# Decoder on one core: a new order of the 16-head part's small operations, with three places behind each pair of products instead of one per slot

## What is computed

```python
def _L0_attn_ref(x, w_qkv, w_proj):
    qkv = x @ w_qkv
    ...
    q = q * cos + _rotate_half(q) * sin
    k = k * cos + _rotate_half(k) * sin
    attn = jax.nn.softmax(jnp.einsum('bhqd,bhkd->bhqk', q, k) * scale, axis=-1)
    out = jnp.einsum('bhqk,bhkd->bhqd', attn, v)
    ...
    return out @ w_proj
...
x = _layernorm(x + _L0_attn_ref(x, L0_attn_w_qkv, L0_attn_w_proj), axis=-1)
x = _layernorm(x + _L0_xattn_ref(x, ctx_1024, ctx_1024, ...), axis=-1)
```

## Time and profile before

| | |
|---|---|
| median of three runs | 2249.5 us (2247.09 to 2249.76) |
| the profiled execution | span 2234.3 us; its own device time is not listed apart from the three runs, whose median is 15.2 us over the span |
| PE busy | 2109.7 us (94%) |
| DVE, ACT, POOL busy | 1661.7, 1501.9, 1327.5 us |
| copies | 248.92 MB, mean 111 GB/s |
| chain that ended last | PE 77%, copies 5%, POOL 5%, SP's queue 4%, ACT 3%, DVE 3% |

### The profile page before, as it was taken

The page is one execution under the profiler, slowest core; times in us unless marked ns, Lnnn a source line. Parts: engine busy times, 40 slices in busy tenths (PEclk is TensorE's granted clock), DMA queues, the critical chain, the costliest instruction groups (busy, mean ns, idle before and its releaser), DMA issues.

```text
span 2234.3 us, 44819 instructions
## 1 busy us (share of the span) xinstructions
PE 2109.7 (94%) x13992; PEld 1475.9 (66%) x13992; DVE 1661.7 (74%) x3987; ACT 1501.9 (67%) x3418; POOL 1327.5 (59%) x1376
## 2 busy tenths in 40 slices
PE   3899999999999999977999999899989999998998
PEld 2544444444444444346888888788878888887887
DVE  4777888777888888747888888656388888886675
ACT  2287777777888888855777777554367777775443
POOL 0344555533334444477888877454378887875775
PEclk7699999999999999999999999999999999999999
DMA  7667677665756666434545455300055554552111
GB/s 154 109 125 147 140 146 137 144 143 124 154 136 155 159 160 137 140 101 105 131 109 115 103 115 110 93 26 6 1 138 116 111 113 107 108 114 62 58 62 43
DMA packets 201337, 248.92 MB, mean 111 GB/s; under 512 B 26584, under 2 KB 119512, under 8 KB 201112
## 3 DMA queue, kind: packets, MB, share of 16 engines
q1 hardware_dynamic: 198552, 237.68, 47.7%
q0 software_dynamic: 2560, 8.39, 1.1%
HBM read 97.47 MB, written 63.44 MB: 72 GB/s over the span
## 4 chain that ended last, share of the span: by engine, by line
PE 77%; DMA 5%; POOL 5%; SPq 4%; ACT 3%; DVE 3%; issue 2%; POOLq 0%; ACTq 0%; DVEq 0%
PE PS L485 14%; PE PS L487 12%; PE PS L486 12%; PE PS L606 9%; PE PS L590 8%; PE PS L573 5%; PE PS L699 5%; PE PS L675 5%; PE PS L684 4%; DMA KS<-hs 3%; PE PS L659 2%; SPq L1496 2%; SPq L1464 1%; ACT PT L827 1%; DMA hs<-HL 1%
## 5 line engine op out<-in xcount | busy, mean ns | idle before, releaser
L1003 DVE TENSOR_REDUCE MX<-PS 128x1 f32<-128x512 f32 x1024 | 642.5, 682 | 167.1 <-PE PS L573 156.9
L827 ACT ACTIVATE PT<-PS 128x512 f32<-128x512 f32 x1024 | 546.2, 599 | 129.5 <-PE PS L590 127.6
L573 PE MATMUL PS<-KS,QS 48*128 48x512 f32 x1024 | 357.0, 454 | 43.7 <-DMA KS<-hs 33.5
L590 PE MATMUL PS<-QS,KS 50*128 50x512 f32 x1024 | 385.5, 456 | 6.4 <-ACT PT L827 6.0
L590 PEld LDWEIGHTS PS<-QS,KS 50*128 50x128 f32 x1024 | 164.9, 187 | 270.5 <-issue 212.3
L1369 POOL TENSOR_TENSOR PB<-PB,RC 128x512 f32<-128x512 f32 (+1 forms) x256 | 250.6, 999 | 48.6 <-DVE RC L1123 48.6
L606 PE MATMUL PS<-PT,VP 128*17 128x512 f32 x2048 | 273.6, 606 | 2.9 <-ACT OT L834 2.9
L890 ACT ACTIVATE PB<-PB,NMf 128x256 f32<-128x256 f32 (+1 forms) x512 | 242.6, 478 | 8.6 <-DVE NMf L1114 8.5
L573 PEld LDWEIGHTS PS<-KS,QS 48*128 48x128 f32 x1024 | 171.5, 192 | 108.0 <-issue 59.3
L1349 POOL TENSOR_TENSOR RI<-RI,mhalf 128x8 f32<-128x8 f32 x128 | 214.1, 1672 | 10.7
L1114 DVE CUSTOM_DVE_ANT_0 PB<-PS,mk 128x256 f32<-128x256 f32 (+1 forms) x512 | 175.7, 385 | 54.4 <-PE PS L675 54.2
(11 more groups left out here) (182 smaller groups left out, 5054.4 us busy)
## 6 DMA issues: line engine op xcount, KB each, us to landing
qT<-QN SPq DMA_DIRECT2D x384, 128.0 KB, 2.4
hs<-HL SPq DMA_DIRECT2D x64, 512.0 KB, 3.8
kT<-kT SPq DMA_DIRECT2D x256, 128.0 KB, 2.5
QS<-hs SPq DMA_DIRECT2D x192, 128.0 KB, 5.9
KS<-hs SPq DMA_DIRECT2D x192, 128.0 KB, 8.0
od<-OT SPq DMA_DIRECT2D x64, 256.0 KB, 5.9
OC<-od SPq DMA_DIRECT2D x32, 256.0 KB
cst<-rs SPq DMA_DIRECT2D x32, 256.0 KB
```

The source lines that it names most:

```text
L573: pe.matmul(PS[:, bank, :], QS[rows, s, h // 2, qt * P:(qt + 1) * P], KS[rows, s, h // 2, :], start=True, stop=True).then_inc(fills("amax" ...
L590: pe.matmul(PS[:, bank, :], KS[rows, s, pair, kt * P:(kt + 1) * P], QS[rows, s, pair, :], start=True, stop=True).then_inc(fills("score", v ...
L827: act.activation(PT[:, kt % 2, 2 * i + half], PS[:, TURNS["score", vb, g, kt, half, i][0], :], ACT.Exp).then_inc(drains("score", vb, g, kt ...
L1003: dve.tensor_reduce(MX[:, vb % 2, h // 8, qt, c:c + 1], PS[:, TURNS["amax", vb, h, qt][0], :], AX, ALU.max).then_inc(drains("amax", vb, h, ...
```

## The change

Both tables are written anew. A place is now a number from 0 to 95, three for each slot: `3 * slot` is behind the slot's first pair of products, `3 * slot + 1` behind the second, and `3 * slot + 2` behind the `pv` (in odd slots; in even ones it's the same as the place before it). `LAG` is 16 units, the distance between `amax` and `score` that there was. `LAST_STEP` keeps its order and is only renumbered. `stats` gets one wait, because the two halves' lags are no longer the same. The list holds the same operations as before, 7866 of them.

The core of the diff, without the tables but for a few rows:

```diff
 SELF_ORDER = (
-    (1, "stats", (1,), 4), (1, "ot", (3,), 2), (1, "spread", (), 3), (2, "val", (0,), 0), (2, "val_out", (0,), 0), (2, "val_out", (1,), 0),
-    (2, "ot_out", (2,), 2), (2, "val", (1,), 0), (2, "tr_hi", (0,), -1), (2, "tr", (0,), -1), (2, "tr", (1,), -1), (2, "tr_lo", (0,), -1),
...
+    (1, "proj", (0,), 4), (1, "res", (0,), 4), (2, "scale", (0,), 3), (2, "proj", (1,), 4), (2, "res", (1,), 4), (4, "ot", (3,), 2),
+    (4, "stats", (0,), 4), (5, "val_out", (0,), 0), (5, "val_out", (1,), 0), (5, "val", (0,), 0), (5, "val", (1,), 0), (6, "tr_hi", (0,), -1),
...
@@ -108,45 +109,53 @@
     out = []
     orders = [(range(0, NB), SELF_ORDER), (range(NB, NV), CROSS_ORDER)]
     lags = [k for _, order in orders for _, _, _, k in order]
+    first = {s[0] for s in FIRST_BATCH} | {"load_xt", "stack"}
     out += [(s[0], 0) + s[1:] for s in FIRST_BATCH] + [("split_w", 0, 2), ("split_w", 0, 3)]
     out += [("load_x", 2), ("load_bias",)]
-    for step in range(min(lags), NV + 1):
-        a, b = step, step - 1
-        at = [[] for _ in range(32)]
+    last = {(kind,) + part for _, kind, part in LAST_STEP} | {s for stages in LAST_BATCH.values() for s in stages}
+    places = {}
+
+    def put(step, place, stage):
+        places.setdefault(96 * step + place, []).append(stage)
+
+    for step in range(min(lags), NV + max(lags)):
         for batches, order in orders:
-            for slot, kind, part, k in order:
+            for place, kind, part, k in order:
                 vb = step - k
-                if vb == 0 and (k < 0 or kind == "stack"):
+                if vb not in batches or vb == 0 and kind in first or (kind, vb) + part in last:
                     continue
-                if vb in batches and (step < NV or k in (0, 1) or vb == NV - 4):
-                    at[slot].append((kind, vb) + part)
-                    if vb == NB - 1 and (kind, part) == ("rope", (1, 1)):
-                        at[min(slot + 3, 31)] += [("load_w", 1, 0), ("load_w", 1, 1)]
-                        at[min(slot + 11, 31)] += [("split_w", 1, 0), ("split_w", 1, 1)]
-                    if vb == NB - 1 and (kind, part) == ("val", (1,)):
-                        at[slot + 3].append(("load_w", 1, 2))
-                        at[slot + 11].append(("split_w", 1, 2))
+                put(step, place, (kind, vb) + part)
+                if vb == NB - 1 and (kind, part) == ("rope", (1, 1)):
+                    for j in range(2):
+                        put(step, place + 9, ("load_w", 1, j))
+                        put(step, place + 33, ("split_w", 1, j))
+                if vb == NB - 1 and (kind, part) == ("val", (1,)):
+                    put(step, place + 9, ("load_w", 1, 2))
+                    put(step, place + 33, ("split_w", 1, 2))
         if 0 <= step and step + 3 < NB:
-            at[12].append(("load_x", step + 3))
+            put(step, 38, ("load_x", step + 3))
         if step == 2:
-            at[10].append(("load_w", 1, 3))
-            at[30].append(("split_w", 1, 3))
+            put(step, 32, ("load_w", 1, 3))
+            put(step, 92, ("split_w", 1, 3))
         if step == 3:
-            at[20].append(("fold",))
-        if step == NV:
-            for slot, kind, part in LAST_STEP:
-                at[slot].append((kind,) + part)
-        for slot in range(32):
-            g, k, half = slot // 8, slot // 2 % 4, slot % 2
+            put(step, 62, ("fold",))
+    for slot, kind, part in LAST_STEP:
+        put(NV - 1, 3 * slot + 2, (kind,) + part)
+    for n in range(16 * min(lags), 16 * NV + LAG + 1):
+        for half in range(2):
+            slot = 2 * n + half
             for i in range(2):
-                both = [("score", b, g, k, half, i), ("amax", a, 4 * g + 2 * i + 1 - half, k)]
+                a, b = n, n - LAG
+                both = [("score", b // 16, b // 4 % 4, b % 4, half, i), ("amax", a // 16, 4 * (a // 4 % 4) + 2 * i + 1 - half, a % 4)]
                 out += [s for s in (both if half == 0 else both[::-1]) if 0 <= s[1] < NV]
-            if half:
-                n = 16 * b + 4 * g + k - 1
-                if 0 <= n < 16 * NV:
-                    out.append(("pv", n // 16, n // 4 % 4, n % 4))
-            out += at[slot]
-    return out + [("pv", NV - 1, 3, 3)]
+                out += places.pop(3 * slot + i, ())
+            if half and 0 <= n - LAG - 1 < 16 * NV:
+                p = n - LAG - 1
+                out.append(("pv", p // 16, p // 4 % 4, p % 4))
+            out += places.pop(3 * slot + 2, ())
+    for place in sorted(places):
+        out += places[place]
+    return out
 
 
 
@@ -1025,6 +1034,8 @@
             def stats(vb, half):
                 n, T = 2 * vb + half, LNT[:, half]
                 dve.wait_ge(*drained("proj", vb, half))
+                if vb:
+                    dve.wait_ge(sem["normed"], 2 * vb + half - 1)
                 for i in range(2):
                     dve.bn_stats(T[:, 6 * i:6 * i + 6], X[:, vb % NB, 2 * half + i]).then_inc(sem["stats"], 1)
                 for i in range(2):
```

More of the change, by code:

```diff
@@ L20 @@
 NEG = -3.0e38
+LAG = 16
 def f(ap):
@@ L37 @@
[L37 to L40, removed]
@@ new lines @@
+    (44, "mix_sum", (1, 0), -1), (47, "heads_out", (1, 0), -1), (48, "mix_sum", (1, 1), -1), (48, "heads_lo", (0, 1), -1),
+    (49, "heads_lo", (1, 0), -1), (50, "heads_out", (1, 1), -1), (53, "ot", (1,), 1), (53, "inv", (), 2), (54, "scale", (1,), 3),
+    (55, "heads_lo", (1, 1), -1), (57, "out_lo", (0,), 3), (57, "collect", (0,), 2), (57, "maxrows", (0,), 0), (60, "negmax", (0,), 0),
+    (61, "maxtr", (0,), 0), (62, "stack", (0,), -1), (62, "out_lo", (1,), 3), (68, "inv_out", (), 2), (68, "maxrows", (1,), 0),
@@ new lines @@
+    (10, "tr_lo", (1,), -1), (11, "scale", (1,), 3), (12, "stack", (1,), 0), (15, "bias1_out", (0, 0), -1), (15, "bias1", (0, 0), -1),
+    (17, "heads_hi", (0, 0), -1), (18, "heads_lo", (0, 0), -1), (19, "bias1", (0, 1), -1), (19, "maxrows", (1,), 1), (20, "bias1_out", (0, 1), -1),
+    (21, "ctx_hi", (0,), -1), (23, "heads_out", (0, 0), -1), (24, "ctx_hi", (1,), -1), (25, "sums", (), 2), (25, "negmax", (1,), 1),
+    (26, "ctx_lo", (0,), -1), (27, "maxtr", (1,), 1), (28, "ctx_lo", (1,), -1), (28, "heads_lo", (0, 1), -1), (29, "out_lo", (0,), 3),
@@ L65 @@
+    (58, "ot_out", (0,), 1), (60, "stack", (0,), -1), (66, "inv_out", (), 2), (68, "heads_hi", (1, 1), -1), (70, "negmax_out", (0,), 0),
+    (71, "ot_out", (1,), 1), (76, "heads_lo", (1, 1), -1), (78, "inv", (), 2), (78, "ot", (2,), 1), (79, "collect", (0,), 2), (81, "proj", (0,), 3),
+    (83, "res", (0,), 3), (84, "rstd", (0,), 3), (85, "norm", (0,), 3), (85, "scale", (0,), 2), (92, "collect", (1,), 2), (93, "spread", (), 2),
+    (94, "stats", (0,), 3),
 )
@@ L88 @@
-    (30, "proj", (NV - 2, 1)), (26, "res", (NV - 2, 1)), (26, "stats", (NV - 2, 1)), (26, "rstd", (NV - 2, 1)), (26, "norm", (NV - 2, 1)),
-) + tuple((13 + k if k < 4 else 19 + k, "split_qkv", (0, k)) for k in range(10)) + (
-    (31, "ot_out", (NV - 1, 2)), (31, "collect", (NV - 1, 0)),
+    (32, "spread", (NV - 3,)), (32, "ot_out", (NV - 2, 2)), (32, "load_consts", ()), (32, "load_qkv", (0, None)),
+    (34, "ot", (NV - 2, 3)), (35, "ot_out", (NV - 2, 3)), (35, "sums", (NV - 2,)), (35, "collect", (NV - 2, 0)), (35, "collect", (NV - 2, 1)),
@@ new lines @@
+    (49, "scale", (NV - 2, 0)), (49, "scale", (NV - 2, 1)), (55, "out_hi", (NV - 2, 0)), (55, "out_lo", (NV - 2, 0)),
+    (56, "out_hi", (NV - 2, 1)), (56, "out_lo", (NV - 2, 1)), (56, "add_bo", (NV - 1,)),
+    (60, "proj", (NV - 2, 0)), (56, "res", (NV - 2, 0)), (56, "stats", (NV - 2, 0)), (56, "rstd", (NV - 2, 0)), (56, "norm", (NV - 2, 0)),
+    (62, "proj", (NV - 2, 1)), (58, "res", (NV - 2, 1)), (58, "stats", (NV - 2, 1)), (58, "rstd", (NV - 2, 1)), (58, "norm", (NV - 2, 1)),
+) + tuple((45 + k if k < 4 else 51 + k, "split_qkv", (0, k)) for k in range(10)) + (
+    (63, "ot_out", (NV - 1, 2)), (63, "collect", (NV - 1, 0)),
```

55 lines of the change are left out of this document (21 added, 34 removed).

## The result

The changed kernel took 2220.75 us (median of 4 runs, 2219.4 to 2226.31) beside 2248.3 us before (2237.82 to 2249.76, 4 runs): ratio 0.9893, 95% interval 0.9869 to 0.9916. The forecast was 2230 with a range of 2216 to 2251, faster with 0.77. The traced execution's span is 2218.3 us, and the same execution took 2220.51: 2.2 us lie outside the span.

The account below looks back on a forecast made before the run. TensorE (PE) was taken to bound the kernel, busy 2109.7 of 2234.3 us. Terms of -5.1 (steps 2, 3), +0.6 (4 to 6), -6.4, -6.8, -4.2 and +2.5 gave -19.4 from 2249.5: 2230 us, range 2216 to 2251.

Parts of the forecast that it names:

- The maxima: Change from self to cross steps: PE's 2.40 us waits for maxima rows go; step 7 -6.4, step 8 -6.8.
- The transposes: Self steps: the 0.66 us wait for VectorE's cast goes, 1.1 us less a 0.2 switch; -0.9, to 54.1.
- The stack: Head copies for the next batch's first maxima: 1.0 us late in every self step, making these 52.4 or 55.1.
- with less queued ahead I take 15.4: Twelve stack copies in a self step: from start to use 15.4 us, where it was 16.1.
- The negated maxima: Their copy to the query rows, now behind the stack on SP's queue: 0.3 us late, lower bound 0.
- over 1 us: Sign of being wrong: PE waiting this long for the negated maxima.
- The clock: Half clock behind 1 us waits: 1.4 us among steps 1 to 3 and 1.4 among 4 to 6.
- Projections at no cost to PE, 2.7 us to come back: Self-half output projections moved to the next step's head: PE pays nothing; 2.7 us return in step 11 and the last step.
- Cross steps: Steps 9 to 14: a lone transpose's wait goes, less 0.2 for a cast; 6 x 0.7, -4.2 us.
- The median lies 15.2 over the span, which stays: Whole kernel: median of runs 2249.5 us against profiled span 2234.3, a gap assumed unchanged.
- Slower: Rival: stack and maxima miss PE by over 1.6 us each self step and the clock falls; 2260 us, chance 0.12.
- New waits of ScalarE that eat half: Rival: ScalarE's early casts and value copies delay exponentials, 0.7 us in each of 14 steps; 2240 us, chance 0.20.

Follow-up runs that it names:

- the second trace: The changed kernel itself run again, nothing altered, beside more runs of the kernel before: 2218.27 us, ratio 0.9877.
- Experiment 1: Kernel before, with only the second half's maxima rows of a self batch moved to the end of their own step: 2234.84 us, ratio 0.9984.
- experiment 2: Kernel before with maxima rows early, and both self-half transposes one slot later: 2240.31 us, ratio 1.0011.
- experiment 4: Changed kernel with the negated maxima and both stores of the value sums ahead of the stack copies on SyncE's queue: 2253.37 us, ratio 1.0056.
- 11: Changed kernel with one 256 KB store of the value sums ahead of the stack on SyncE's queue instead of behind it: 2219.36 us.
- experiment 7: Kernel before with maxima rows early, one store of the value sums moved behind the stack copies, the other 8 slots earlier: 2241.58 us, ratio 0.9967.
- experiment 3: Changed kernel with the first half's negated maxima of a self batch copied ahead of the twelve stack copies: 2214.85 us, ratio 0.9892.
- Experiment 8: Changed kernel with the self half's two output projections back near the end of the step before: 2211.74 us, ratio 0.9844.
- experiment 12: Changed kernel with a self step's transposes straight behind the value projections again, casts unmoved: 2244.33 us, ratio 0.9987.
- experiment 10: Changed kernel with self projections late, negated maxima ahead of the stack, and two of four last-batch score products per unit made twice: 2211.42 us.

## Why the prediction was right, and where it was not

- **The maxima (-13.2 for steps 7 and 8): right, -12.9,** and -10.0 in the second trace, where step 7 had the late negated maxima. Experiment 1 shows the mechanism alone; the other 2.4 us of step 7's gain needed the stack in time as well (58.04 us there, 55.65 in the changed kernel).
- **The transposes (-0.9 a self step): right in kind, a little less in size.** The wait is gone, and steps 4 and 5 are at 54.3 and 54.6 (54.3 and 54.3 in the second trace), from 55.0 in the mean, where 54.1 was forecast without the stack. The reason was half of it. Four products between are not enough by themselves (experiment 2); the reader of the cast has to be far too.
- **The stack (1.0 us late in every self step): wrong, it was never late.** The start was right (41.2 forecast, 41.9 and 41.4 measured). The term that failed is "with less queued ahead I take 15.4": issuing and the slowest flight took 12.9 us in step 5 and 13.8 in step 3. I read the 16.1 us of the earlier trace rows as nearly the copies' own and did not ask what was queued ahead of them. Experiments 4 and 11 put stores back there, and over steps 2 to 5 the slowest copy took 9.3 and 9.2 us in the mean, where the changed kernel's two traces have 8.2 and 8.1 and six variants of it without a store just ahead 7.5 to 8.9. In the kernel before it was 10.5, and experiment 7, without the stores ahead, still had 9.6 where experiment 1, with them, had 9.7. So the queue ahead is at most one part of it, and the other stays open. Steps 4 to 6 gave -3.3 for my +0.6, and this is most of the difference.
- **The negated maxima (+0.3): right in the mean, not in kind.** It was 0.58 and 0.87 us in two of six steps in the first trace, 0.20 and 2.20 in the second. The 2.20, and 6.27 us ahead of step 1, where I had not looked, are the "over 1 us" that I had named as a sign of being wrong. PE's waits for these copies ended behind the stack's last landing (202.80 us after 202.02, 420.62 after 420.37), and in experiment 3, with them ahead of it, no step waited for them. The rule that I had weighed, ring order in the Trainium skill (DMA: Bandwidth & Descriptors, section on queues, rings and completion order), agrees with these numbers. But "cannot pass" was more than it gives: the same section says that a later descriptor may finish its write before an earlier one.
- **The clock (+2.8): not needed in the first trace,** where every step from 2 to 14 reads 1.00; in the second one fall in step 7.
- **Projections at no cost to PE, 2.7 us to come back: right.** Experiment 8 puts them back and the step's length stays. (What the earlier trace rows price at 1.30 us are six matmuls, `project` in the kernel, and not the twelve that the description of the kernel gives a `rope`; the sums are not touched.) The 2.7 us reappear in step 11 (357 matmuls for 346) and in the last step.
- **Cross steps (-4.2): measured -1.6,** or -2.9 without the projection that came back.
- **"The median lies 15.2 over the span, which stays": wrong.** It is 2.2 to 2.4 in every run. The traced execution of before took some 2236.6 us and was among the faster ones: 10 of the 61 later runs were below that. With this gap my -19.4 would have led to 2217. So some 13 us of the forecast were a misreading of one trace. What stood against them was the last two steps, for which I had only part of the 2.7 us of projections to come back and which took 11.7 more, mostly at half clock, while the rest of the head part gained more than forecast. That the time lies well inside the range is partly luck. In the last score step the clock falls for over 20 us in two of the four traces on the old order (experiments 1 and 7), for 3.4 us in experiment 2, not in the trace of before, and in all ten on the new one. Whether the new order makes it likelier stays open, as so few traces can't tell.
- **The rivals.** Slower was to decide at an arrival over 1.6 us late; experiment 4 is that case, and it came out at 2253, with 14 us of waits in it that the case did not have. New waits of ScalarE that eat half did not show.

No single part of the change is shown to carry the gain. Early maxima alone, with the transposes or with a store moved, give a ratio of 0.997 to 1.001, while the trace of experiment 1 has 9.7 us less in two steps. Experiments 4 and 12 lose all of the gain, but neither is a clean reversal: one brings 14 us of waits of its own, the other waits of 1.86 us for the old 0.66.

What the traces show is the sum. PE's waits of 0.4 us and more in steps 2 to 14 add up to 14.3 us before and to 2.1 and 2.2 in the changed kernel's two traces. The other orders fall in line: 10.4 us and a median of 2235 in experiment 1, 12.8 and 2242 in 7, 14.0 and 2240 in 2, 13.5 and 2244 in 12, 24.0 and 2253 in 4, and 1.7 to 4.8 us with 2211 to 2219 in the rest. The clock is the smaller part. Take the runs whose mean granted clock was 0.969 to 0.971: the 14 of before lie at 2232.83 to 2240.71 us, the four of the changed kernel at 2217.46 to 2220.99, 18 us less in the mean. So some 18 of the 27 us between the medians are there at equal clock, 12 of them such waits; the other 6 I cannot assign. This compares runs and is no experiment on the clock, as a mean over the span does not say where it was low.

## What to carry to other kernels

Give each small operation of an in-order engine distance both to what it waits for and to what waits for it: moving the transposes away from one neighbour alone made a longer wait at the other. Where a wait of the bounding engine can also cost its clock, count the waits themselves first; here they fell by 12 us, and the clock is left with some 9 of the 27 us at most. A copy's time to landing changed by 1 to 3 us with the order around it, so read it afresh for each order. And compare the traced execution's own time with the runs before adding a gap between span and median; with a spread of 36 us, one trace of before is a sample.

## What was not expected of the hardware

- The spread of one program. Sixty-one runs of before lie within 36 us, and their time follows the mean granted clock: from 0.975 (2226.67 us) to 0.956 (2259.08) is 32 us. The changed kernel's ten lie within 10.
- That a wait's length alone does not tell whether the clock falls. In the fourteen traces, steps 2 to 15, no wait of PE of 0.4 to 0.92 us had a fall to 0.50 in it or within 2 us behind it, and all 14 of 1.89 us and more had one. Of the 32 waits between, 18 had one and 14 had none. The shortest with a fall was 0.94 us (experiment 4, step 4), the longest without one 1.81 (experiment 12, step 7), and 1.74 us went both ways (experiment 10, step 3, and experiment 8, step 14). The steps that read 0.97 with one such fall lost another 1.3 to 2 us by it.
